# Cross-attention on one core: one transfer for each weight chunk and its bias columns, and the weighing of Wk by bq on GpSimd

## What is computed

```python
q = emb @ Wq + bq;  k = latent @ Wk + bk;  v = latent @ Wv + bv
w = (q @ k.T) * E**-0.5            # 100 x 722
w = softmax(w, axis=0)             # over the 100 rows of q, not over the context
x = w @ v + emb
out = (x - mean(x)) * rsqrt(var(x) + 1e-6) * gamma + beta
```

## Time and profile before

| | |
|---|---|
| median of the runs | 151.87 us (151.82 to 151.93) |
| the profiled execution's own time | 151.6 us |
| its span, first to last instruction | 149.8 us |
| busy: TensorE / VectorE / ScalarE / GpSimd | 93% / 80% / 57% / 58% |
| granted TensorE clock | 0.992 of full |
| transfers over the span | 247 GB/s |

### The profile page before, as it was taken

How to read it: one execution, slowest core, us unless ns; L and a number is a source line. 1 busy time by engine, 2 the same in 40 slices (tenths; PEclk the granted TensorE clock), 3 DMA queues, 4 the chain that set the end, 5 groups by cost and what they waited for, 6 DMA issues and landing times.

```text
span 149.8 us, 3112 instructions
## 1 busy us (share of the span) xinstructions
PE 138.9 (93%) x1070; PEld 130.7 (87%) x1070; DVE 119.8 (80%) x227; ACT 85.8 (57%) x292; POOL 87.5 (58%) x78
## 2 busy tenths in 40 slices
PE   7899999899899999999999999999999999999900
PEld 7789999798898989999998989899998989897700
DVE  0799989699777888779697978779697968777981
ACT  4468365289527937575573938475573938474410
POOL 0350049809032495866849494856749494859880
PEclk9999999999999999999999999999999999999996
DMA  4999659998065579889888989999888984653123
GB/s 136 296 352 418 275 154 285 377 293 322 25 209 198 193 285 334 288 267 306 265 263 305 267 321 280 322 257 335 263 260 284 285 308 122 241 190 114 55 69 95
DMA packets 11336, 37.14 MB, mean 248 GB/s; under 512 B 1422, under 2 KB 1934, under 8 KB 11322
## 3 DMA queue, kind: packets, MB, share of 16 engines
q1 hardware_dynamic: 9714, 34.50, 69.1%
q10 hardware_dynamic: 1608, 2.46, 4.6%
HBM read 33.68 MB, written 3.28 MB: 247 GB/s over the span
## 4 chain that ended last, share of the span: by engine, by line
PE 70%; DVE 14%; POOL 6%; DMA 3%; issue 2%; ACT 1%; SPq 1%; POOLq 1%; DVEq 0%
PE ps_U L372 27%; PE ps_S L358 26%; PE ps_Y L391 12%; DVE xu L624 6%; PE ps_U L333 3%; POOL result L810 3%; DMA wkT<-WkT 3%; DVE xT_lo L612 2%; POOL resid L800 2%; DVE wq_lo L598 2%; DVE wkq L604 1%; DVE W_lo L708 1%; PE ps_w L381 1%; POOL prob L790 1%; ACT xu_hi L483 1%
## 5 line engine op out<-in xcount | busy, mean ns | idle before, releaser
L494 ACT ACTIVATE expo<-scores,negmax 121x100 f32<-121x100 f32 x96 | 35.0, 366 | 26.6 <-DVE negmax L644 26.6
L358 PE MATMUL ps_S<-G,ctxT_in 128*121 128x100 f32 (+1 forms) x384 | 43.7, 270 | 0.6 <-DVE scores L640 0.6
L372 PEld LDWEIGHTS ps_U<-prob,ctx_in 121*128 121x128 f32 x360 | 42.4, 192 | 1.5
L358 PEld LDWEIGHTS ps_S<-G,ctxT_in 128*121 128x121 f32 (+1 forms) x384 | 41.9, 185 | 0.9 <-issue 0.9
L372 PE MATMUL ps_U<-prob,ctx_in 121*128 121x100 f32 x360 | 42.4, 274 | 0.0
L804 POOL TENSOR_TENSOR rstd<-vareps,neg_half 100x1 f32<-100x1 f32 x16 | 15.4, 960 | 27.5 <-DVE vareps L680 25.5
L790 POOL TENSOR_TENSOR prob<-expo,rinv 121x600 f32<-121x600 f32 x16 | 19.0, 1189 | 9.0 <-DVE rinv L651 9.0
L800 POOL TENSOR_TENSOR resid<-x_in,bvw 100x512 f32<-100x512 f32 x16 | 20.4, 1273 | 4.6 <-ACT bvw L511 4.4
L640 DVE TENSOR_TENSOR scores<-ps_S,c_rows 121x600 f32<-121x600 f32 x16 | 12.5, 782 | 13.2 <-issue 11.8
L657 DVE TENSOR_REDUCE probsum<-prob 121x100 f32<-121x600 f32 x16 | 19.8, 1239 | 1.0 <-POOL prob L790 0.6
L810 POOL TENSOR_TENSOR result<-scaled,beta_rows 100x512 f32<-100x512 f32 x15 | 19.3, 1291 | 0.0
(11 more groups left out here) (92 smaller groups left out, 184.1 us busy)
## 6 DMA issues: line engine op xcount, KB each, us to landing
ctx_in<-ctx SPq DMA_DIRECT2D x16, 768.0 KB, 6.4
ctxT_in<-ctxT SPq DMA_DIRECT2D x16, 722.0 KB, 6.6
xT_in<-xT SPq DMA_DIRECT2D x8, 400.0 KB, 5.9
x_in<-x SPq DMA_DIRECT2D x16, 200.0 KB
out<-result ACTq DMA_DIRECT2D x12, 200.0 KB
wqT<-WqT SPq DMA_DIRECT2D x4, 256.0 KB, 3.4
out<-result SPq DMA_DIRECT2D x3, 200.0 KB
wkT<-WkT SPq DMA_DIRECT2D x4, 128.0 KB, 3.9
```

What stands on the lines that cost most here:

```text
L358: last = nc.tensor.matmul(ps_scores(c)[0:rows(c), :], ctxT_in[:, q, l * M + c * MP:l * M + c * MP + rows(c)], G[:, l, bass.ds(b * T, T)], ...
L372: last = nc.tensor.matmul(ps_U[:, q, l * T:(l + 1) * T], ctx_in[0:rows(c), q, c, l * P:(l + 1) * P], prob[0:rows(c), q, c * T:(c + 1) * T] ...
L494: last = nc.scalar.activation(expo[0:MP, q, c * T:(c + 1) * T], scores[0:MP, q, c * T:(c + 1) * T], ACT.Exp, bias=negmax[0:MP, q, c:c + 1] ...
```

## The change

The host lays Wq^T, Wk^T, bk (twice) and bq side by side in one array `Wqk`, 776 columns of which 771 are used, so that each chunk is one transfer of 128 rows of 3104 bytes into `wqk`. The names `wqT`, `wkT` and `bq_col` become views of it. Gone are four transfers on SyncE, two on ScalarE's queue, the copy of bk (L592) and its semaphore. VectorE no longer weighs Wk: GpSimd does that after its four `wk_lo`, with one product of all four chunks at once (128 x 4 x 257, bq repeated along the last axis) and two additions (514, then 257 columns), each waiting for the one before. The results lie in the buffers `expo` and `prob`, which are not in use so early. The two readers, L411 on TensorE and L715 on VectorE, wait for the third of these steps.

```diff
@@ sync
             for c in range(EC):
-                sp.dma_start(wqT[:, c, :], WqT[c]).then_inc(w_in[c], 16)
-                sp.dma_start(wkT[:, c, 0:L], WkT[c]).then_inc(w_in[c], 16)
+                sp.dma_start(wqk[:, c, :], Wqk[c]).then_inc(w_in[c], 16)
@@ tensor
-            pe.wait_ge(wkq_step, EC)
+            pe.wait_ge(wkq_step, 3)
...
@@ scalar
-                act.dma_start(bk_in[:, :], bk.rearrange("(p c) -> p c", c=EC)).then_inc(bk_loaded, 16)
-                act.dma_start(bq_col[:, :], bq.rearrange("(p c) -> p c", c=EC)).then_inc(bq_loaded, 16)
...
@@ vector
-            dve.wait_ge(bk_loaded, 16)
-            nc.vector.tensor_copy(wkT[:, :, L:L + 2], bk_in[:, :].unsqueeze(2).to_broadcast([P, EC, 2])).then_inc(bkcol_set, 1)
-            dve.wait_ge(bkcol_set, 1)
             for c in range(EC):
-                dve.wait_ge(w_in[c], 32)
+                dve.wait_ge(w_in[c], 16)
                 nc.vector.tensor_copy(wk_hi[:, c, :], wkT[:, c, :]).then_inc(wkhi_set, 1)
                 dve.wait_ge(wqhi_set, c + 1)
                 nc.vector.tensor_tensor(wq_lo[:, c, :], wqT[:, c, :], wq_hi[:, c, :].bitcast(F32), ALU.subtract).then_inc(wqlo_set, 1)
-                if c == 0:
-                    dve.wait_ge(bq_loaded, 16)
-                    nc.vector.tensor_scalar(wkq[:, 0, :], wkT[:, 0, :], bq_col[:, 0:1], None, ALU.mult).then_inc(wkq_step, 1)
-                else:
-                    dve.wait_ge(wkq_step, c)
-                    nc.vector.scalar_tensor_tensor(wkq[:, c % 2, :], wkT[:, c, :], bq_col[:, c:c + 1],
-                                                   wkq[:, (c - 1) % 2, :], ALU.mult, ALU.add).then_inc(wkq_step, 1)
@@ gpsimd
             for c in range(EC):
...
                 nc.gpsimd.tensor_tensor(wk_lo[:, c, :], wkT[:, c, :], wk_hi[:, c, :].bitcast(F32), ALU.subtract).then_inc(wklo_set, 1)
+            nc.gpsimd.tensor_tensor(wkq[:, :, :], wkT[:, :, 0:L + 1], bq_col[:, :, :].to_broadcast([P, EC, L + 1]),
+                                    ALU.mult).then_inc(wkq_step, 1)
+            pool.wait_ge(wkq_step, 1)
+            nc.gpsimd.tensor_tensor(wkq2[:, :, :], wkq[:, 0:2, :], wkq[:, 2:4, :], ALU.add).then_inc(wkq_step, 1)
+            pool.wait_ge(wkq_step, 2)
+            nc.gpsimd.tensor_tensor(wkq1[:, :], wkq2[:, 0, :], wkq2[:, 1, :], ALU.add).then_inc(wkq_step, 1)
             nc.gpsimd.memset(mask[:, :], 1.0).then_inc(mask_set, 1)
```

More of the change, by code:

```diff
@@ L28, with xattn @@
 MC_CHUNKS = 6
-def xattn(nc, xT, x, ctxT, ctx, WqT, WkT, bq, bk, Wv, bv, gamma, beta, out):
+def xattn(nc, xT, x, ctxT, ctx, Wqk, Wv, bv, gamma, beta, out):
     B, T, E = x.shape
@@ L60, in xattn @@
         WARM = 9
-        wqT = sb("wqT", [P, EC, E])
-        wkT = sb("wkT", [P, EC, L + 2])
+        wqk = sb("wqk", [P, EC, Wqk.shape[2]])
         wq_hi = sb("wq_hi", [P, EC, E], F32R)
@@ L68, in xattn @@
         wk_lo = sb("wk_lo", [P, EC, L + 2], F32R)
-        bk_in = sb("bk_in", [P, EC])
-        wkq = sb("wkq", [P, 2, L + 2])
-        bq_col = sb("bq_col", [P, EC])
         W_hi = sb("W_hi", [P, EC, L], F32R)
@@ L141, in xattn @@
         onesr_set = sem("onesr_set")
-        bkcol_set = sem("bkcol_set")
         wqhi_set = sem("wqhi_set")
@@ L196, in xattn @@
         result_set = sem("result_set")
+        wqT = wqk[:, :, 0:E]
+        wkT = wqk[:, :, E:E + L + 2]
+        bq_col = wqk[:, :, E + L + 2:E + L + 3]
+        wkq2 = prob[:, 0, 0:2 * (L + 1)].rearrange("p (c l) -> p c l", l=L + 1)
+        wkq1 = prob[:, 1, 0:L + 1]
+        wkq = expo.rearrange("p q n -> p (q n)")[:, 0:EC * (L + 1)].rearrange("p (c l) -> p c l", l=L + 1)
         def rows(c):
@@ L407, in _ @@
             project(0)
-            pe.wait_ge(wkq_step, EC)
+            pe.wait_ge(wkq_step, 3)
             for c in range(LC):
-                last = nc.tensor.matmul(ps_w[:, c:c + 1], wkq[:, (EC - 1) % 2, c * P:(c + 1) * P], ones[:, 0:1],
+                last = nc.tensor.matmul(ps_w[:, c:c + 1], wkq1[:, c * P:(c + 1) * P], ones[:, 0:1],
                                         start=True, stop=True)
@@ L457, in _ @@
         def _(act):
-            with nc.allow_non_contiguous_dma("small constants"):
-                act.dma_start(bk_in[:, :], bk.rearrange("(p c) -> p c", c=EC)).then_inc(bk_loaded, 16)
-                act.dma_start(bq_col[:, :], bq.rearrange("(p c) -> p c", c=EC)).then_inc(bq_loaded, 16)
             def upper_half(g):
@@ L539, in _ @@
             for f in range(EC):
-                act.wait_ge(w_in[f], 32)
+                act.wait_ge(w_in[f], 16)
                 nc.scalar.activation(wq_hi[:, f, :], wqT[:, f, :], ACT.Copy).then_inc(wqhi_set, 1)
@@ L712, in _ @@
             lower_half(1)
-            dve.wait_ge(wkq_step, EC)
-            nc.vector.tensor_scalar(bb_col[:, :], wkq[:, (EC - 1) % 2, L:L + 1], SCALE, None, ALU.mult).then_inc(bb_set, 1)
+            dve.wait_ge(wkq_step, 3)
+            nc.vector.tensor_scalar(bb_col[:, :], wkq1[:, L:L + 1], SCALE, None, ALU.mult).then_inc(bb_set, 1)
             dve.wait_ge(bb_set, 1)
@@ L773, in _ @@
         def _(pool):
-            pool.wait_ge(bkcol_set, 1)
             for c in range(EC):
-                pool.wait_ge(w_in[c], 32)
+                pool.wait_ge(w_in[c], 16)
                 pool.wait_ge(wkhi_set, c + 1)
                 nc.gpsimd.tensor_tensor(wk_lo[:, c, :], wkT[:, c, :], wk_hi[:, c, :].bitcast(F32), ALU.subtract).then_inc(wklo_set, 1)
+            nc.gpsimd.tensor_tensor(wkq[:, :, :], wkT[:, :, 0:L + 1], bq_col[:, :, :].to_broadcast([P, EC, L + 1]),
[4 more added lines that the diff above has]
+            nc.gpsimd.tensor_tensor(wkq1[:, :], wkq2[:, 0, :], wkq2[:, 1, :], ALU.add).then_inc(wkq_step, 1)
             nc.gpsimd.memset(mask[:, :], 1.0).then_inc(mask_set, 1)
@@ L878 @@
     ctx_p[:, 0:MP] = rows.reshape(B, MC_CHUNKS, MP, L).transpose(0, 2, 1, 3).reshape(B, MP, MC_CHUNKS * L)
+    Wqk = np.zeros((EC, P, E + L + 8), x.dtype)
+    Wqk[:, :, 0:E] = np.asarray(L0_xattn_Wq).T.reshape(P, EC, E).transpose(1, 0, 2)
+    Wqk[:, :, E:E + L] = np.asarray(L0_xattn_Wk).T.reshape(P, EC, L).transpose(1, 0, 2)
+    Wqk[:, :, E + L] = np.asarray(L0_xattn_bk).reshape(P, EC).T
+    Wqk[:, :, E + L + 1] = np.asarray(L0_xattn_bk).reshape(P, EC).T
+    Wqk[:, :, E + L + 2] = np.asarray(L0_xattn_bq).reshape(P, EC).T
     arrays = {
@@ L884 @@
         "ctx": ctx_p,
-        "WqT": np.ascontiguousarray(np.asarray(L0_xattn_Wq).T.reshape(P, EC, E).transpose(1, 0, 2)),
-        "WkT": np.ascontiguousarray(np.asarray(L0_xattn_Wk).T.reshape(P, EC, L).transpose(1, 0, 2)),
-        "bq": np.asarray(L0_xattn_bq),
-        "bk": np.asarray(L0_xattn_bk),
+        "Wqk": Wqk,
         "Wv": np.asarray(L0_xattn_Wv),
```

2 lines of the change are left out of this document (removed).

## The result

The changed kernel takes 155.20 us (median of six runs, 153.43 to 156.23), the kernel before beside it 151.84 (six runs, 151.69 to 152.21). The ratio is **1.0183, with a 95% interval of 1.0121 to 1.0244**: slower, and beyond the range of the forecast (151.8 to 153.5).

What follows compares the result with a forecast made beforehand. VectorE was taken to lead until batch 0's scores at 28.86, TensorE (busy 93%) after. Its fourth xT_lo, 0.4 us later through GpSimd's blocking, gave 151.87 + 0.4 = 152.3 us, range 151.8 to 153.5.

Steps and rivals of the forecast that it cites:

- What VectorE gains or loses before 28.86 passes on to the end one for one: Start up to batch 0's scores: VectorE leads, so its change reaches the end, gains up to 0.62 us plus TensorE's own.
- The transfers: Weight loads at the start: chunk 3 used at 7.25 instead of 8.07, first half of xT at 8.8.
- The casts wait: VectorE's wk_hi copies wait for a running GpSimd wk_lo; otherwise the fourth wk_lo ends at about 9.4.
- The fourth `wk_lo` at 9.9, the product of 2.15, the turns: GpSimd's last wk_lo, then its 2.15 us product, alternating with VectorE's xT_lo; the second xT_lo ends at 13.6.
- 0.13 to 0.15 of the prediction: VectorE and GpSimd turns: an instruction that waited saves some 0.13 to 0.15 us of its length at the hand-over.
- the predicted +0.4: VectorE's fourth xT_lo ends at 17.2 instead of 16.80, so the whole kernel is 0.4 us slower.
- Rival A: GpSimd's product starts ahead of VectorE's first xT_lo: +1.0 to +1.8 us, 152.9 to 153.7; chance 0.27.
- Rival C: GpSimd's product doesn't block VectorE's xT_lo, so the fourth ends 1.5 us sooner: 150.4 us; chance 0.09.
- The granted clock ... is taken as unchanged: TensorE's clock: it stood at 1.00 (2.4 GHz) even before the second chunk, so no change was counted.
- Scores of batch 0 near 29.3, wait before batch 1 of 0.62 or more: Signs in the new profile: VectorE's batch 0 scores near 29.3, TensorE's wait before batch 1's scores at least 0.62 us.

Runs made afterwards that it cites:

- h4: The kernel before with Wv, bv, gamma and beta listed ahead of WqT, WkT, bq and bk, no instruction changed; 155.73 us, ratio 1.0259.
- e4: The changed kernel with the ctxT_in transfer for batch 2 issued ahead of ctx_in and x_in of batch 1; 152.51 us, ratio 1.0021.
- e1: The kernel before with only the weighing moved to GpSimd, its transfers as before; 153.52 us, ratio 1.0099.
- e3: The changed kernel with the four old arrays kept unused in their places in the input list and Wqk last; 152.06 us, ratio 1.0006.

## Why the prediction was wrong

The forecast was 152.3 us, in the range of 151.8 to 153.5; measured is 155.2. Its direction was right by luck: the reason that it gave holds nearly nothing of the loss.

**The step that failed** is "What VectorE gains or loses before 28.86 passes on to the end one for one": VectorE lost nothing (its scores began at 28.82, where it was 28.86), and the end came 3.52 us later. The step takes every transfer behind 28.86 as landing in time; `ctxT_in` of batch 2 landed 3.08 later and held TensorE up for 1.64. It followed the transfers up to 8 us and the turns of VectorE and GpSimd up to 16.80, and never asked which transfer of the next stage has the least in hand. That is `ctxT_in` of batch 2: 38.7 - 37.2 = 1.5 us. Nor did it list as an edit that four input arrays become one. No row of the profile before could have priced that (h4 shows 2.6% for it); but the small margin was there to see, and would have given a rival "a later transfer becomes the wait" its place, if not its price.

Point by point:

- *The transfers.* Chunk 3 was predicted for use at 7.25, the first half of xT at 8.8. ScalarE's timeline has them at 7.29 and 8.57:

```profile
7.29 0.64 ACT L536 ACTIVATE wq_hi<-wqk 128x512 fp32r<-128x512 f32 x1 [0.37 <-DMA wqk<-Wqk]
8.57 1.88 ACT L463 ACTIVATE xT_hi<-xT_in 128x800 fp32r<-128x800 f32 x2 [0.64 <-DMA xT_in<-xT]
```

- *The casts wait.* Taken without a row, and right: 0.73 and 0.83 us beside a GpSimd `wk_lo`, where one alone takes 0.30. VectorE of the changed kernel, and below it the two `wk_lo` that they wait for, which end at 7.27 and 8.62:

```profile
6.69 0.73 DVE L588 CAST wk_hi<-wqk 128x258 fp32r<-128x258 f32 x1
7.95 0.83 DVE L588 CAST wk_hi<-wqk 128x258 fp32r<-128x258 f32 x1
```

```profile
6.31 0.96 POOL L762 TENSOR_TENSOR wk_lo<-wqk,wk_hi 128x258 fp32r<-128x258 f32 x1 [0.90 <-DVE wk_hi L588]
7.57 1.05 POOL L762 TENSOR_TENSOR wk_lo<-wqk,wk_hi 128x258 fp32r<-128x258 f32 x1 [0.30 <-DVE wk_hi L588]
```

The Trainium skill (SBUF — State Buffer, Who interferes with whom) says so of VectorE's copies and casts, and these rows agree.

- *The fourth `wk_lo` at 9.9, the product of 2.15, the turns.* GpSimd of the changed kernel, and below it VectorE:

```profile
8.92 0.96 POOL L762 TENSOR_TENSOR wk_lo<-wqk,wk_hi 128x258 fp32r<-128x258 f32 x1 [0.30 <-DVE wk_hi L588]
9.84 2.66 POOL L763 TENSOR_TENSOR expo<-wqk 128x1028 f32<-128x1028 f32 x1
...
14.38 0.64 POOL L768 TENSOR_TENSOR prob<-prob 128x257 f32<-128x257 f32 x1
```

```profile
9.48 1.25 DVE L597 TENSOR_TENSOR xT_lo<-xT_in,xT_hi 128x800 fp32r<-128x800 f32 x1
10.65 2.69 DVE L597 TENSOR_TENSOR xT_lo<-xT_in,xT_hi 128x800 fp32r<-128x800 f32 x1
```

The fourth `wk_lo` ends at 9.88. The product takes 2.66 here, as it ran beside the first `xT_lo` until 9.48 + 1.25 = 10.73, and ends at 12.50, 1.77 behind it (12.75 was predicted); e4 has it unhindered at 2.36, within the bounds of 1.9 to 2.4 and above the 2.15 taken. So an instruction that waited saved 0.59 of its length here, and not the 0.13 to 0.15 of the prediction; e1 has the same (13.53 - 11.77 = 1.76). Why it saves so much isn't shown. The second `xT_lo` takes 2.69, held as predicted. But it ends at 13.34 and not at 13.6, and the second addition is done at 14.38 + 0.64 = 15.02, where 15.45 was predicted, so that the third `xT_lo`, started at 14.86, was hardly held: it and the fourth took 1.91 us together. With that the predicted +0.4 became 16.77 - 16.80 = 0.0. e3, which is the change without the array effect, fits this with 1.0006, though its interval (0.9981 to 1.0031, some -0.3 to +0.5 us) doesn't exclude the +0.4; it is the traces that show the term as 0.4 too high (e3's fourth `xT_lo` ends at 16.68). And the sum lacked a term of over 3 us.

- *Rival A* was the order in e4, at +1.0; of the 13 profiles with the product only that one has it. e1's +1.0 is another thing: the order of the prediction's own case, without the earlier transfers. *Rival C* is excluded: the second `xT_lo` is held by the product in all 13.
- *"The granted clock ... is taken as unchanged"*: wrong. Its fall gave 1.74 of the 3.52 us.
- *Scores of batch 0 near 29.3, wait before batch 1 of 0.62 or more.* VectorE's scores began at 28.82 (28.86 before), and the wait is 1.06, as TensorE was done sooner (27.07 + 1.62 = 28.69, 29.16 before).

## What to carry to other kernels

Before a change to an early stage is priced, list for each later stage the transfer with the least time in hand, and take as a rival that it comes late: here 1.5 us in hand was spent, and the wait of 1.64 us was followed by a fall of the clock that cost 1.74 more. Count the list of input arrays among the edits, and when one changes, run the new program once with the old list (unused arrays in the old places): that takes the effect of the list out of the comparison. Work that was moved from VectorE to GpSimd wasn't off VectorE's path, as both read two operands from SBUF (an `xT_lo` took 2.69 us instead of 0.98); merged transfers with the weighing left where it was gave the only gain.
